# A transformer layer on 8 cores: one projection group moved to the seam between FFN blocks, one wait per PSUM bank, and an earlier bias addition

## The reference, cut to what matters

```
qkv  = x @ c_attn.T + b_attn                      # 16 heads of 64
attn = causal softmax(q k^T / 8) v
x    = layernorm(x + attn @ c_proj.T + b_proj)
h    = gelu(x @ w1 + b1)                          # 1024 -> 4096
out  = layernorm(x + h @ w2 + b2)                 # 4096 -> 1024
```

## Time and profile before

| | us |
|---|---|
| median of 3 runs | 2309.55 |
| the 3 runs | 2304.05, 2309.55, 2389.6 |
| the profiled execution, its own time | 2304.15 |
| its span on core 2, the slowest | 2302.6 |
| spans of the eight cores | 2290.1 to 2302.6 |

### The profile page before, as it was taken

How to read it: one execution, slowest core, us unless ns; L and a number is a source line. 1 busy time by engine, 2 the same in 40 slices (tenths; PEclk the granted TensorE clock), 3 DMA queues, 4 the chain that set the end, 5 groups by cost and what they waited for, 6 DMA issues and landing times.

```text
span 2302.6 us, 65004 instructions; the slowest of 8 cores (2290.1 to 2302.6 us)
## 1 busy us (share of the span) xinstructions
PE 2099.2 (91%) x30242; PEld 1304.1 (57%) x30242; DVE 751.1 (33%) x1925; ACT 1343.1 (58%) x1666; POOL 218.3 (9%) x181
## 2 busy tenths in 40 slices
PE   7988998998989989888778899999999999999997
PEld 3444654655555565444445566666666666666665
DVE  3444334334343433432212133223222233223221
ACT  2777996999999999999996122222222222222222
POOL 2000000000000000000111322111011122111010
PEclk8999999999999999999899999999999999999999
DMA  9600100001000000000782311111100111111000
GB/s 147 94 16 8 29 7 18 10 10 30 10 19 12 7 21 10 5 17 25 147 138 58 58 46 46 47 47 46 46 19 28 47 47 46 47 46 46 19 19 19
DMA packets 52624, 89.72 MB, mean 39 GB/s; under 512 B 3200, under 2 KB 35968, under 8 KB 51328
## 3 DMA queue, kind: packets, MB, share of 16 engines
q0 software_dynamic: 16784, 33.56, 9.7%
q1 hardware_dynamic: 35568, 52.00, 6.7%
HBM read 93.94 MB, written 25.17 MB: 52 GB/s over the span
## 4 chain that ended last, share of the span: by engine, by line
PE 60%; ACT 30%; DVE 6%; DMA 2%; issue 1%; POOL 0%; POOLq 0%; SPq 0%; DVEq 0%
ACT work L566 30%; PE ps L951 19%; PE ps L933 18%; PE ps L410 5%; PE ps L618 5%; PE ps L768 4%; PE ps L549 4%; DVE qkv L445 2%; DVE work L968 2%; PE ps L366 1%; PE ps L273 1%; DMA xT<-xb 1%; PE ps L462 1%; DMA qkv<-w 1%; PE ps L811 1%
## 5 line engine op out<-in xcount | busy, mean ns | idle before, releaser
L566 ACT ACTIVATE work<-ps,cb 128x1024 bf16<-128x1024 f32 (+3 forms) x1152 | 1097.8, 1089 | 120.0 <-PE ps L549 114.7
L941 ACT ACTIVATE work<-ps,b_s 128x256 bf16<-128x256 f32 x512 | 242.8, 474 | 794.7 <-PE ps L933 794.7
L618 PEld LDWEIGHTS ps<-qkv,work 64*128 64x128 bf16 x16896 | 444.1, 95 | 282.5 <-PE ps L618 74.8
L618 PE MATMUL ps<-qkv,work 64*128 64x65 bf16 x16896 | 588.1, 192 | 7.7 <-DVE work L643 4.3
L951 PE MATMUL ps<-qkv,work 128*128 128x512 bf16 x2048 | 527.1, 380 | 19.8 <-DVE work L968 19.5
L933 PE MATMUL ps<-work,xT 128*128 128x256 bf16 x4096 | 532.7, 273 | 0.4 <-issue 0.4
L549 PE MATMUL ps<-qkv 64*128 64x512 bf16 (+3 forms) x2304 | 428.3, 369 | 103.1 <-ACT work L566 97.5
L933 PEld LDWEIGHTS ps<-work,xT 128*128 128x128 bf16 x4096 | 401.7, 98 | 156.7 <-issue 1.0
L951 PEld LDWEIGHTS ps<-qkv,work 128*128 128x128 bf16 x2048 | 198.3, 98 | 208.7 <-DVE work L968 26.7
L410 PE MATMUL ps<-xT,work 64*128 64x512 bf16 x896 | 272.2, 379 | 3.3 <-DVE stat L467 2.3
L411 PE MATMUL ps<-xT,work 64*128 64x512 bf16 x896 | 272.4, 379 | 0.0
(11 more groups left out here) (58 smaller groups left out, 1125.2 us busy)
## 6 DMA issues: line engine op xcount, KB each, us to landing
work<-x SPq DMA_DIRECT2D x16, 1024.0 KB, 5.1
out<-work SPq DMA_DIRECT2D x16, 1024.0 KB, 4.0
attn_s<-work SPq DMA_DIRECT2D x64, 128.0 KB, 1.8
xT<-w POOLq DMA_DIRECT2D x8, 1024.0 KB, 15.4
work<-attn_s SPq DMA_DIRECT2D x16, 512.0 KB, 6.4
qkv<-w POOLq DMA_DIRECT2D x16, 512.0 KB, 8.7
xT<-xb POOLq DMA_DIRECT2D x7, 1024.0 KB, 45.8
work<-wqk POOLq DMA_DIRECT2D x7, 512.0 KB, 6.5
```

What stands on the lines that cost most here:

```text
L566: lambda: sc.activation(pb, ps, AF.Exp, bias=cb[:, 8 * p + g : 8 * p + g + 1], scale=0.125),
L618: r = t.matmul(bank(6 + h)[:, 65 * c : 65 * c + 65], pbuf[i % NP][rows, 512 * h + 128 * c : 512 * h + 128 * c + 128], w[rows, o : o + 65], ...
L941: lambda: sc.activation(hbuf[ui % 4], bank(4 + ui % 2)[:, 0:TB], AF.Gelu, bias=b1[:, hc : hc + 1]),
```

## The change

Four things are altered. The bias addition of block 1 moves to the last pair, behind that of block 0 and ahead of the w1 loads. At the seam between blocks, the first projection group of the block after next is issued before the banks' additions are waited for: its 8 matmuls stand between the first product of unit 1 and the rest, its DVE addition stands behind the four additions that empty the banks, and the other three groups (`rest`) begin at `hc` 0 as before. Block 1's four groups stay where they were, from `hc` 4 of block 0; at the seam from block 14 to 15 there is no group left to move. The second product of unit 0 waits for each bank separately, before that bank's matmul. The last block's output is stored in two halves, each as soon as it is scaled.

```diff
@@ attention, last pair, first group of queries
                 add_bias(0)
+                add_bias(1)
                 load_w1()
@@ start of the FFN stage
     load_w2(8, 16, end_pe, t_at[1])
     load_block(2)
-    add_bias(1)
@@ put_f2
-        tok = pe.put(go, t_h[ui], ld_w2[hc // 2], *(f2_free if hc == 0 else ()))
+        if hc == 0:
+            for k in range(4):
+                c, oh = divmod(k, 2)
+                tok = pe.put(
+                    lambda k=k, c=c, oh=oh: t.matmul(
+                        bank(k), hbuf[ui % 4][:, 128 * c : 128 * c + 128],
+                        w2[hc][:, 512 * oh : 512 * oh + 512], start=True, stop=False),
+                    f2_free[k], t_h[ui], ld_w2[0], mark=k == 3)
+        else:
+            tok = pe.put(go, t_h[ui], ld_w2[hc // 2])
@@ finish is cut in two: empty_banks(b, tok) has the four additions, finish(b, sts) the norms
+            if b == NB - 1:
+                r = TB * b + 128 * c
+                sp.dma(slot(f"st{n}"), out_d[r : r + 128, :], y, fin[c])
+        if b < NB - 1:
+            st_out[b] = sp.dma(...)
@@ loop over units
         if hc == (4 if b == 0 else 0) and b + 1 < NB:
-            extra.extend(proj_steps(b + 1))
+            extra.extend(rest if b else proj_steps(b + 1))
@@ at hc 31, after put_f2(ui) and put_f1(ui + 2)
-            finish(b, tok)
+            steps = proj_steps(b + 2) if b + 2 < NB else []
+            for c, go in steps[:7]:
+                go()
+            sts = empty_banks(b, tok)
+            for c, go in steps[7:8]:
+                go()
+            rest = steps[8:]
+            finish(b, sts)
             load_block(b + 3)
```

More of the change, by code:

```diff
@@ L955, in go, with empty_banks @@
             return a, r
-        tok = pe.put(go, t_h[ui], ld_w2[hc // 2], *(f2_free if hc == 0 else ()))
+        if hc == 0:
[8 more added lines that the diff above has]
+            tok = pe.put(go, t_h[ui], ld_w2[hc // 2])
         h_free[ui % 4] = tok
         return tok
-    def finish(b, tok):
+    def empty_banks(b, tok):
         n = b % 3
@@ L971, in finish @@
             sts.append(ys)
+        return sts
+    def finish(b, sts):
+        n = b % 3
         fin = []
@@ L977, in finish @@
                 lambda y=y, scl=scl, sft=sft: v.tensor_scalar(y, y, scl, sft, ALU.mult, ALU.add), nm))
-        st_out[b] = sp.dma(slot(f"st{n}"), out_d[TB * b : TB * b + TB, :].rearrange("(c p) f -> p c f", p=128),
-                           xbuf[n].rearrange("p (c f) -> p c f", c=2), *fin)
+            if b == NB - 1:
+                r = TB * b + 128 * c
+                sp.dma(slot(f"st{n}"), out_d[r : r + 128, :], y, fin[c])
+        if b < NB - 1:
+            st_out[b] = sp.dma(
+                slot(f"st{n}"), out_d[TB * b : TB * b + TB, :].rearrange("(c p) f -> p c f", p=128),
+                xbuf[n].rearrange("p (c f) -> p c f", c=2), *fin)
     extra = deque()
```

## The result

The changed kernel takes 2276.05 us (median of 4 runs) against 2308.06 us (4 runs) of the kernel before. The ratio is 0.9863, 95% interval 0.9834 to 0.9891: 1.4% faster, less than the 2% that the forecast took as its border. 2273 had been forecast. The ratios here leave out executions in which one die ran at a lower clock than the other, and those are also why some medians lie above what the ratio says. The profiled execution takes 2278.44 us, its slowest core is core 4 with a span of 2276.9 us.

What follows compares the result with a forecast made beforehand. ACT bounds the attention stage, PE the FFN stage, where only waits can be won. 2304.15 - 20.8 (seams, banks) - 10.3 (block 1's bias) + 1.5 (masks) - 1.3 (tail) = 2273.2 us; range 2262 to 2289.

Steps and rivals of the forecast that it cites:

- The sum: Whole kernel: the profiled execution's 2304.15 us less 20.8, 10.3 and 1.3, plus 1.5, giving 2273.2 us.
- FFN terms: Gains forecast in the FFN stage: 20.8 us at seams and banks, 10.3 for block 1's bias, 1.3 at the tail.
- part 3: Block 0, addition of block 1's bias: PE's 7.43 us wait and 2.91 us of low clock behind it go, 10.3 us.
- Part 1: Seams between blocks: eight projection matmuls cover PE's wait for bank-emptying additions, 14 gaps of 1.44 us, 20.2 us.
- Part 2: Second product at seams: separate bank waits give nothing at 14 seams, 0.65 us saved at the last.
- Part 4: Last attention pair: masks slowed beside the moved POOL bias addition cost 1.5 us, between 0 and 2.9.
- The Trainium skill's rule: VectorE instructions with two SBUF inputs and GpSimd ones reading SBUF exclude each other; would make the sum 3.2 us worse.
- Part 5: Last block's output: storing two halves, the first gone before the second is ready, gains 1.3 us, between 0 and 2.2.
- I expect core 2 to stay last: Across cores: core 2 remains slowest; core 4, winning only seams and tail, would give 2278 us.
- A: Block 0: its wait comes back in another form (w2 pair, power behind POOL's list, another core); 2283.5 us, chance 0.14.
- B: Every block: the chain through POOL reaches PE and makes the kernel slower, 2417 us; chance 0.03.
- C: Seam: the moved group itself waits (bank 6 or attention rows), only moving the gap; 2293 us, chance 0.05.

Runs made afterwards that it cites:

- the bias alone: Kernel before with only the bias addition of block 1 moved to the last pair, behind that of block 0; ratio 0.9972 to before.
- the kernel with one wait: Changed kernel, but the second product of unit 0 waits for all four banks at once; ratio 0.9876 to before.
- bias elsewhere: Changed kernel with the bias addition of block 1 behind the first half of w2's loads; whole ratio 0.9876, first L727 to first L933 141.6 us.
- memsets in place of useless additions: Kernel with block 1's bias behind half of w2, plus two POOL memsets in the early place (other kernel: two unneeded additions); first L727 to first L933 142.2 us.
- small loads: Changed kernel loading only 64 columns of each w1 part and 32 of each in w2's first half; first L727 to first L933 142.0 us.
- four matmuls and bank waits: Changed kernel with 4 projection matmuls of the group at the seam in place of 8, wait per bank kept; FFN stage 1022.9 us.

## Why the prediction was right, point by point

**The sum, and the luck in it.** 2273 was forecast and 2276 measured. The sum was core 2's, and on the mean of the cores it was too high: 30.9 us forecast, 25.3 gained between the profiled executions. 2.3 of the 5.6 us are FFN terms (32.4 forecast, 30.1 measured, the difference in part 3), 3.3 are the attention stage (1.5 and 4.8). Yet by the ratio of 0.9863 the slowest core gained 31.6 us, 0.7 more than the sum. The wait in block 0, long on some cores and short on others, had set the cores apart, and the change took that spread away with it. No term had this, so it is in part luck that the total came so close.

**Part 1, the group at the seam: right.** 14 gaps of 1.44 us were forecast to go. Blocks follow each other every 63.38 us in place of 64.82, and the earlier trace rows have their answer without a gap. From the additions of the first seam to those behind the last block it was 964.07 us and is 943.16, so parts 1 and 2 gave 20.9 us, against 20.8. Between the bias alone and the changed kernel the FFN stage went from 1045.3 to 1022.8 us, 22.5 us for parts 1, 2 and 5, against 22.1.

**Part 2, the wait per bank: right.** Nothing at the 14 seams; at the last one 0.65 us by the trace of the kernel with one wait, 0.65 forecast. By starts and pace 1.2 us of waiting are left there (2.96 - 2 x 0.87), against the forecast's 1.1; the 0.4 us of the view of waits is modelled idle time and so shorter. The three additional waits have no price that shows, since blocks follow each other at the same distance with them and without.

**Part 3, the bias of block 1: right, and larger than the wait it removes.** The wait and the half clock behind it went. Core 2's FFN stage fits to 0.1 us. What the term did not say is that it is core 2's: the wait was 1.5 to 9.8 us by core, the mean gain of the FFN stage 5.6 to 7.5 us in place of 10.3, and since the core that is last changes from run to run, no single core's sum is the kernel's.

**Part 4, the masks: the step that was mis-sized.** I took 1.5 us between 0 and 2.9, and the stretch rose by 3.7 us, from 139.8 to 143.5 (144.1 once more). The mechanism held, and for the masks so did the bounds: PE's waits for them rose from 0.15 to 2.4 us on the mean of the cores, and the stretch differs by 1.9 us (bias elsewhere) and 2.6 us (memsets in place of useless additions) where they go. I had set half of the upper bound, and the second addition stands beside the next group's masks on every core, so it is held nearly in full. What no term had is the rest, 1.1 to 2.4 us: the stretch is 141.6 and 142.2 us without any wait for masks. With small loads, where masks are held and the stalls are gone, it is 142.0 us, 2.2 above the kernel before and so about what the masks cost. So the rest seems to go with the loads. But no run has small loads and the bias in its old place, and the sums of the stalls, 1.5 and 1.8 us with the bias there and 1.6 to 3.4 with it moved, overlap. The cause of the rest stays open; the half clock behind each stall is a candidate that I did not measure by itself. The Trainium skill's rule ("SBUF — State Buffer", section "Who interferes with whom") is borne out in both halves by the runs: a pair of masks took 2.00 us beside an addition that reads SBUF, and beside a memset, which only writes, the 0.36 us that it takes alone. The 4.7 us that the prediction worked out by that rule is more than masks cost here.

**Part 5, the tail: right.** 1.4 us against 1.3; 512 KB land in 2.8 us against 2.7 interpolated.

**The slowest core.** "I expect core 2 to stay last" was wrong. The FFN stage no longer tells the cores apart, so the last is the one whose attention stage was longest. Often it is one with a long issue stall: core 4 (4.8 us) in the profiled execution of the changed kernel, core 1 (7.3 us) in that with the bias behind half of w2. It need not be: with one store it was core 0, which had no such stall and 3.7 us of waits for masks. The profiled execution lies 5 us above the sum: core 4's first L933 came at 1254.3 us, where the sum has 1248.9 for core 2, and its stall is most of that.

**The rivals.** A (block 0's wait comes back) did not happen: no wait for w2 and none for the power of the first norm. B had its mechanism but not its effect. DVE does stand longer behind POOL:

```profile
1409.63 0.16 DVE L743 SCALAR_TENSOR_TENSOR lnst<-lnst 128x1 f32<-128x1 f32 x1 [12.63 <-POOL lnst L741]
1409.83 0.81 DVE L789 TENSOR_SCALAR work<-work,lnst 128x1024 bf16<-128x1024 f32 x1
...
1426.96 0.61 PE L811 MATMUL ps<-idb_s,work 128*128 128x128 bf16 x8
```

12.6 us of standing in every steady block, 4.1 us before, and all of it free, because the turn that needs L789 comes 17 us later. DVE stands longer because it is ready earlier, not because POOL is late: counted from the seam's additions L789 starts 25.19 us behind them, 24.52 before, so 0.67 us later, where the forecast saw 0.7. C did not happen: no group at a seam waits; the one wait of L768 left in the FFN stage is 0.9 us on core 3 (0.3 on core 7), for the attention rows of block 1 in block 0.

No experiment beat the changed kernel by more than the measurement can tell. The kernels with the bias behind half of w2 and with four matmuls and bank waits (one execution) are its equals.

## What to carry to other kernels

Price a wait by starts and pace, then put work of at least that length in front of it that has to be done anyway: here 1.74 us of matmuls removed the whole gap of 1.44 us per seam, and 0.87 us of them left exactly 0.57. Waits per bank pay only when the work in front is shorter than the emptying of all banks. When an instruction of POOL is moved off one path, look at what DVE does in its new place: a cheap addition beside masks with two SBUF operands gave back 2 us of the 5.6 to 7.5 that its move had won. And when one stage is made equal on all cores, the slowest core is picked by what differs in the other.

## What the runs showed of the hardware that I had not expected

- PE's issue stalls. While the weight loads keep the DMA engines 90% busy, PE stands for up to 7.3 us at a time with nothing to wait for that the profile shows, though not on every core; with the DMA share at 0.16 the longest is 0.3 us (one execution). A stall of 4.8 us is followed by a stretch at half clock (granted 0.50).
- A wait of 7.4 us on PE cost 10.3: the granted clock was 0.54 for 6.4 us behind it, and removing it gave core 2 what the forecast had. Gaps of 1.44 us at the seams left it at 1.00 (from 1388 to 1393 us in the kernel before).
